# Flipped half tiles of a DLRM tower go through DRAM instead of from SBUF to SBUF

## The reference

```
e = jnp.stack([tbl_0[ids[:, 0]], ..., tbl_26[ids[:, 26]]], axis=1)
z = jnp.einsum('bnd,bmd->bnm', e, e)[:, i, j]      # i < j
h = jnp.concatenate([z.reshape(z.shape[0], -1), dense_ctx], axis=1)
h = jnp.maximum(h @ W_top1 + b_top1, 0.0)
h = jnp.maximum(h @ W_top2 + b_top2, 0.0)
y = h @ W_top3
```

## Time and profile before

| | |
|---|---|
| median of three runs | 444.68 us (444.11 to 446.41) |
| profiled execution | 444.69 us, its span 442.9 us |
| TensorE matmul busy | 341.5 us, 77% |
| VectorE busy | 246.3 us, 56% |
| ScalarE busy | 199.4 us, 45% |
| GpSimd busy | 242.6 us, 55% |
| moved by DMA | 55.09 MB |
| mean granted clock of TensorE | 0.903 |

### The profile page before, as it was taken

The page is one execution under the profiler, slowest core; times in us unless marked ns, Lnnn a source line. Parts: engine busy times, 40 slices in busy tenths (PEclk is TensorE's granted clock), DMA queues, the critical chain, the costliest instruction groups (busy, mean ns, idle before and its releaser), DMA issues.

```text
span 442.9 us, 8208 instructions
## 1 busy us (share of the span) xinstructions
PE 341.5 (77%) x3310; PEld 281.3 (64%) x3310; DVE 246.3 (56%) x202; ACT 199.4 (45%) x294; POOL 242.6 (55%) x263
## 2 busy tenths in 40 slices
PE   3999893759994989629896789809899489718767
PEld 2677793547872877428774678508786379717666
DVE  6899964596185726459266925739247743610100
ACT  5798663125463257113572166212662256322432
POOL 6777777660577637753377727754177737720000
PEclk9999998869999799959999699958999699867889
DMA  7966825562274536754174645844246533732230
GB/s 184 217 163 195 227 76 149 157 152 79 77 176 129 145 91 83 200 126 134 53 166 123 161 99 73 207 113 134 68 105 174 140 79 83 176 89 55 44 62 14
DMA packets 70111, 55.09 MB, mean 124 GB/s; under 512 B 45186, under 2 KB 60111, under 8 KB 70073
## 3 DMA queue, kind: packets, MB, share of 16 engines
q1 hardware_dynamic: 60121, 37.56, 35.4%
q0 software_dynamic: 8192, 16.79, 15.0%
q10 hardware_dynamic: 1760, 0.22, 0.3%
HBM read 36.43 MB, written 7.09 MB: 98 GB/s over the span
## 4 chain that ended last, share of the span: by engine, by line
SPq 45%; PE 30%; issue 10%; DMA 6%; DVE 5%; ACT 3%; ACTq 1%; DVEq 0%
SPq L415 31%; SPq L440 8%; PE emb_ps L625 7%; PE emb_ps L627 6%; PE mlp_ps L672 6%; DVE onehot L798 4%; PE gram_ps L655 4%; DMA moved<-flips 3%; DMA h<-tbl_rows 2%; PE mlp_ps L681 2%; SPq L400 2%; ACT emb L955 2%; PE emb_ps L699 1%; SPq L479 1%; DVE flips L853 1%
## 5 line engine op out<-in xcount | busy, mean ns | idle before, releaser
L596 POOL DMA_INDIRECT rows<-tbl_rows,idx x256 | 241.7, 944 | 147.5 <-issue 74.1
L625 PE MATMUL emb_ps<-onehot,table_hi 125*128 125x512 f32 (+1 forms) x400 | 158.0, 404 | 68.9 <-DVE onehot L798 59.5
L798 DVE TENSOR_TENSOR onehot<-ids_b,row_id 125x2048 fp32r<-125x2048 int32 x72 | 160.0, 2273 | 42.7 <-PE emb_ps L627 32.4
L627 PE MATMUL emb_ps<-onehot,table_lo 125*128 125x512 f32 (+1 forms) x400 | 152.1, 389 | 0.0
L625 PEld LDWEIGHTS emb_ps<-onehot,table_hi 125*128 125x128 f32 x400 | 82.5, 206 | 96.4 <-issue 59.1
L627 PEld LDWEIGHTS emb_ps<-onehot,table_lo 125*128 125x128 f32 x400 | 82.7, 207 | 13.0
L655 PE MATMUL gram_ps<-emb 128*54 128x54 f32 x2048 | 58.1, 216 | 11.2 <-ACT gram L966 10.2
L655 PEld LDWEIGHTS gram_ps<-emb 128*54 128x54 f32 x2048 | 54.9, 132 | 17.4 <-ACT gram L966 11.1
L955 ACT COPY emb<-moved 128x1024 f32<-128x1024 f32 x21 | 42.3, 2016 | 45.1 <-DMA moved<-flips 45.0
L853 DVE STREAM_TRANSPOSE flips<-rows 128x512 f32<-128x512 f32 x42 | 27.3, 689 | 62.0 <-DMA moved<-flips 62.0
L923 ACT COPY held<-emb_ps 128x256 f32<-128x256 f32 x38 | 14.2, 375 | 105.3 <-PE emb_ps L627 105.1
(11 more groups left out here) (51 smaller groups left out, 129.0 us busy)
## 6 DMA issues: line engine op xcount, KB each, us to landing
moved<-flips SPq DMA_DIRECT2D x336, 32.0 KB
ids_b<-ids_onehot SPq DMA_DIRECT2D x33, 256.0 KB, 4.7
products<-gram SPq DMA_DIRECT2D x28, 216.0 KB
gram<-tbl_rows SPq DMA_DIRECT2D x9, 480.0 KB
rows<-tbl_rows,idx POOLq DMA_INDIRECT x256
z<-products SPq DMA_DIRECT2D x14, 126.0 KB
h<-tbl_rows SPq DMA_DIRECT2D x2, 480.0 KB
z<-products SPq DMA_DIRECT2D x7, 112.0 KB
```

What stands on the lines that cost most here:

```text
L596: pool.indirect_dma_start(out=rows[:, bank_number(p, t, n) % ROW_BANKS, f - first, :], out_offset=None, in_=gathered_tables[f], in_offset= ...
L625: nc.tensor.matmul(ps[:, 0:width], table_hi[0:ROWS, k, j, :], columns[:, c, :], start=j == 0, stop=False)
L627: last = nc.tensor.matmul(ps[:, 0:width], table_lo[0:ROWS, k, j, :], columns[:, c, :], start=False, stop=j == ROWS_PER - 1)
L798: nc.vector.tensor_tensor(onehot[0:ROWS, seq % ONEHOT_RING, 0:own * width].rearrange("p (j b) -> p j b", b=width), *operands, ALU.is_equal ...
```

## The change

One half tile was put in place by sixteen transfers of 32 partitions by 1 KB from SBUF to SBUF. Now one transfer stores all of `flips` (128 partitions by 4 KB) in a DRAM buffer `halves`, which has two places, and four transfers load it, each 32 partitions of `moved` by four runs of 1 KB. The loads wait on SP for the store's landing (`half_stored`). DVE's next flip waits for the store and no longer for `moved`. In SP's order something stands between store and loads for two of the three halves: `load_z` for (p,0,1) and one `load_ids` for (p,1,0). Nothing changes on TensorE, ScalarE and GpSimd.

```
+        halves = nc.dram_tensor("halves", (2, P, BLOCKS, HALF_BANKS * TURNS_A_BANK * BLOCK), F32)
...
-        HALF_MOVED = BLOCKS * BLOCKS * 16
+        HALF_MOVED = BLOCKS * 16
...
-            def move_half(p, t, h):
-
+            def store_half(p, t, h):
+
+                sp.wait_ge(flipped, FLIPPED_BY[(p, t, (h + 1) * HALF_BANKS - 1)])
                 number = HALF_NUMBER[(p, t, h)]
-                sp.wait_ge(flipped, FLIPPED_BY[(p, t, (h + 1) * HALF_BANKS - 1)])
+                sp.dma_start(halves[number % 2], flips[:, :, :, :, :].rearrange("p b g f j -> p b (g f j)")
+                             ).then_inc(half_stored, 16)
+
+            def load_half(p, t, h):
+
+                number = HALF_NUMBER[(p, t, h)]
+                sp.wait_ge(half_stored, (number + 1) * 16)
 
                 if number > 0:
                     sp.wait_ge(half_placed, number)
-                for q in range(BLOCKS):
-                    for b in range(BLOCKS):
-                        sp.dma_start(
-                            moved[b * BLOCK:(b + 1) * BLOCK, q, :, :].rearrange("p f j -> p (f j)"),
-                            flips[q * BLOCK:(q + 1) * BLOCK, b, :, :, :].rearrange("p g f j -> p (g f j)")
-                        ).then_inc(half_moved, 16)
+                for b in range(BLOCKS):
+                    sp.dma_start(moved[b * BLOCK:(b + 1) * BLOCK, :, :, :].rearrange("p q f j -> p q (f j)"),
+                                 halves[number % 2, :, b, :].rearrange("(q p) x -> p q x", p=BLOCK)
+                                 ).then_inc(half_moved, 16)
...
                 store_products(p - 1)
-                move_half(p, 0, 1)
+                store_half(p, 0, 1)
                 load_z(p - 1)
+                load_half(p, 0, 1)
                 load_dense(p)
                 for i in ids[2:]:
                     load_ids(i)
                 for i in ahead[0:2]:
                     load_ids(i)
-                move_half(p, 1, 0)
-                for i in ahead[2:]:
+                store_half(p, 1, 0)
+                for i in ahead[2:3]:
+                    load_ids(i)
+                load_half(p, 1, 0)
+                for i in ahead[3:]:
                     load_ids(i)
                 if p < LAST:
-                    move_half(p + 1, 0, 0)
+                    store_half(p + 1, 0, 0)
+                    load_half(p + 1, 0, 0)
                     store_y(p - 1)
...
-                    dve.wait_ge(half_moved, number * HALF_MOVED)
+                    dve.wait_ge(half_stored, number * 16)
```

More of the change, by code:

```diff
@@ L322, in build @@
         flipped = sem("flipped")
+        half_stored = sem("half_stored")
         half_moved = sem("half_moved")
@@ L512, in _ @@
                 load_ids(i)
-            move_half(1, 0, 0)
+            store_half(1, 0, 0)
+            load_half(1, 0, 0)
             for p in range(1, PAIRS):
```

## The result

The changed kernel takes 372.77 us (371.66 to 375.01, three runs), where 444.68 stood. The ratio is 0.838, with an interval of 0.831 to 0.846. The forecast was 392 us with a range of 375 to 420. Six more runs of the same kernel beside a later experiment gave 372.84 us.

What follows compares the result with a forecast made beforehand. VectorE's flips waited for SP to issue sixteen moves, and TensorE for one-hots behind them. 442.9 - 9.6 - 37.6 - 10.9 = 384.8 us, with 5.4 of crowding 390.2, with 1.8 beyond the span 392; range 375 to 420.

Steps and rivals of the forecast that it cites:

- What gains is that flips is free after 5.5 us in place of 12.3: At each half, DVE waits for the store alone, and SP issues 4 us in place of 10.4.
- Loads between 0.65 and 0.86, I take 0.86: On SP's queue, each load from DRAM to moved takes 0.86 us to issue, 3.4 for four.
- the walk: The forecast's pair-by-pair timeline: gains of 9.6 us in pair 1, 37.6 in pairs 2 to 6, 10.9 at the end.
- Products ... take 6.9: On SP's queue in pairs of six lookups, products take 6.9 us to go out, and DVE's second flip waits 2.8.
- S to L: From a pair's first lookups to its layer 1: 22.3 us with five lookups, 29.5 with six including the flip wait.
- Crowding: Fuller DMA, share 0.70 to 0.77, slows products to 6.9 us in three pairs of five lookups: 5.4 us added.
- Landing of the store: After a store's issue of 0.5 us, its 512 KB take 5.0 us to land in DRAM.
- Landing of the loads: After the last of a half's four loads is issued, they land in moved 2.0 us later.
- Clock: TensorE's lower clock after the stall goes with the stall; if it stays, up to 2 us a pair.
- the DRAM leg is quick: Rival, chance 0.15: store lands in 2.6 us, loads issue in 0.65 each, no crowding: 375 us.
- GpSimd as the bound: Rival, chance 0.10: gathers stretch by a tenth, 32 take 43.5 us a pair; 397 to 402 us with the crowded queue.
- The slower side: Rival, chance 0.05: store and reload land in 10 and 5 us, making the kernel about 470 us.

Runs made afterwards that it cites:

- e1: The changed kernel, but VectorE's next flip waits until the four loads have landed in moved, not only the store: 409.2 us, ratio 0.919.
- e3: The changed kernel with sixteen loads a half (32 partitions by 1 KB each) in place of four: 451.2 us, ratio 1.014.
- e2: The changed kernel with eight loads a half (32 partitions by two runs of 1 KB) in place of four: 389.2 us, ratio 0.873.
- e6: The changed kernel with two more gathers in each of pairs 2 to 7, into two tiles that nobody reads: 375.8 us, ratio 0.844.

## Why the prediction was right, and where it was wrong

**What bounded the kernel: right.** The stall of VectorE at the flips, made by SP's issuing and the late release, was most of the 72 us. It fell from 62.0 to 2.7 for the transfer, and TensorE's from 59.5 to 15.1 with it. That all of VectorE's wait would be for the store did not hold: 7.3 us are for gathers. One reading is off: the earlier trace rows counts from the start of the last issue, so "10.4 + 1.9 = 12.3" has the last issue twice. From 230.65 to 240.45 + 1.88 it is 11.7 us.

**"What gains is that flips is free after 5.5 us in place of 12.3 (DVE waits for the store alone), and that SP issues 4 us a half in place of 10.4": right in kind.** e1 takes the first away and loses 36 us, e3 the second and loses 78. The prediction had no price for each alone; they do not add up.

**The step that failed: "Loads between 0.65 and 0.86, I take 0.86, the row with the same number of 1 KB runs: 3.4 for four."** A load is issued in 0.43 us (median of 84), four with the gaps mostly in 1.8, half of the term. I had read it off the z loads, which have nearly as many runs; and I gave the moves' 0.65 as lower bound, which is outside the truth too. e2 restores 3.6 to 4.6 us a half and comes to 389.2 us, 16 of the 19 missing. It also shows tile 1's half as the tight place, in all pairs and not only in those of five. Not all of the 16 us is the term itself: in the walk it is 1.6 us in pair 1 and 3.2 at the end, and the rest comes through the later half.

**"Products ... take 6.9" in pair 5:** they took 4.62, and 5.34 in pair 3. Of 2.8 us of wait at each of these flips none came in pair 5 and 1.7 in pair 3. S to L was 26.5 in pair 5, as the walk without waits had it (26.7), and 28.7 in pair 3.

**Crowding, 5.4 us:** the DMA share did rise to 0.71 to 0.76 as forecast. But the term's step, products that take 6.9 in the pairs of five, did not come: they took 3.6 to 4.4 us, and 4.2 to 4.5 in e2. What grew is the landing of tile 1's store (below). The term itself was also too large by its own rows: 6.9 - 4.9 is 2.0 later and not 2.3, which gives 4.5 us.

**Landing of the store, 0.5 + 5.0 us from the start of its issue:** one number for places that differ. It is 3.1 for the first, where the queue is quiet (59.73, its loads start at 62.82), and 5.0 in the chain below. The stores of (p,1,0), with loads and ids ahead of them in the queue, took 4.5 to 5.8 in the pairs of five until their loads could start, and 7.9, 7.6 and 6.6 in pairs 1, 3 and 5:

```profile
72.40 4.97 DMA halves<-flips
```

```profile
168.38 0.43 SPq L412 DMA_DIRECT2D halves<-flips  x1
...
176.00 1.76 SPq L423 DMA_DIRECT2D moved<-halves  x4
```

So the prediction's sign of being wrong, a landing over 7 us, did come in two of six pairs. The half had cover there, since the loads behind it were quick. The Trainium skill's fit (DMA: Bandwidth & Descriptors, Anatomy of one DMA) gave an estimate of 3.2 us; the page states it for DMAs that GpSimd issues, and this store is SP's. The quiet store agrees with it, the crowded ones do not. Whether its warning on writes to HBM has a part in the long ones, no run here shows.

**Landing of the loads, 2.0 us: too short.** ScalarE's copy of (5,0,1) waits until 256.17 for loads issued until 251.83, 4.3 us. That half has cover. In e1 VectorE has none, and its waits there were 36.3 us where the expectation came to 26 to 32.

**Clock:** taking the lower clock as gone with the stall was right: a granted clock of 0.96 to 1.00 in the windows of pairs 2 to 6, in place of 0.88 to 0.93.

**The sum, in spans:** 390.2 forecast, 373.2 measured. Pair 1 is 3.1 better (L at 90.0 and not 93.1), pairs 2 to 6 take 210.5 in place of 214.9 (4.4), the end is 4.1 shorter (1.6 until the last half is copied, 2.5 behind that), and 5.4 of crowding did not come: 17.0. The 4.4 come nearly all from the pairs of six and their products, not from the loads. The rest of the 19 is that the profiled run was 2.2 us above the median of its kernel.

**The rivals:** "the DRAM leg is quick" (375) is nearest to what came, for its 0.65 an issue more than for its landing of 2.6. It counts 3.2 us less in pair 1, though both stores ahead of that pair's flip land 2.4 earlier there, which takes away the whole wait of 4.1. Its sum is then 373.6, still above the result. GpSimd as the bound did not come (e6). The slower side exists, as e3 shows, but its mechanism is issues, not landing.

## What to carry to other kernels

When a queue's issuing is what an engine waits for, count issues and ask what the consumer really needs before it may go on; a longer way in fewer transfers can be the shorter one. The price of an issue is best read from a transfer of the same kind and shape, since neither the same bytes nor the same number of runs gave it here; where none is there, it deserves the widest bound. And once a stall is gone, look again at what a copy stands in front of: moving ScalarE's half copy behind its four gram copies (with the dense copy) gave 8.6 us more.

## What the runs showed of the hardware

- A load of 32 partitions by four runs of 1 KB from DRAM is issued by SP in 0.43 us, four times the bytes of a move from SBUF to SBUF, which took 0.59 (medians of 84 and of 336). In e3 sixteen loads of 32 by 1 KB take 7.29 us at best, 0.42 each with a gap of 0.04: the bytes of a load don't matter to its issue here, and what lies at the other end does. z loads of 126 partitions by 1 KB take 0.83 each; what makes them dearer was not tried.
- A store of 512 KB to DRAM landed 3.1 us after the start of its issue where little else moved, in 5.0 behind products, and in 7.9 at most behind loads and ids.
- Four loads of 128 KB landed 3.5 to 4.3 us after the end of the last issue, in the five places where ScalarE waited for them.
- Gathers went on at 1.25 us each (0.94 busy and 0.30 of issue between) with a DMA share of 0.50 before and of 0.76 with the change: 241.7 us busy in all, both times.
